# A gated-convolution kernel in a new instruction order, with the memory tokens' products contracted over 128 partitions

## The reference

```python
x = x + attention(_gn(x))     # stage 1
#   xn  = rmsnorm(x) * g1;  q, k, v = w_qkv @ xn         (4 heads of 32 rows)
#   k, v get 4 learned "memory" tokens each; q = softmax over a head's rows, k = softmax over tokens
#   context = k v^T;  out = w_out @ (context^T q) + b_out;  out = rmsnorm(out) * g2
x = x + condconv(_gn(x))      # stage 2
#   pooled = 4 x 4 means;  r = sigmoid(relu(fc(relu(rconv(pooled)))))
#   w = sum_k r[k] * expert_weight[k]      (3 experts, 3 x 3 taps, another filter for each image)
#   out = conv3x3(x, w)
```

## Time and profile before

| | us |
|---|---|
| median of 3 runs (476.15 to 477.4) | 477.28 |
| the profiled execution | 476.64 |
| its span, first to last instruction | 474.9 |
| TensorE busy | 425.4 (90%) |
| VectorE busy | 373.1 (79%) |
| ScalarE busy | 293.3 (62%) |
| GpSimd busy | 253.3 (53%) |

### The profile page before, as it was taken

The page is one execution under the profiler, slowest core; times in us unless marked ns, Lnnn a source line. Parts: engine busy times, 40 slices in busy tenths (PEclk is TensorE's granted clock), DMA queues, the critical chain, the costliest instruction groups (busy, mean ns, idle before and its releaser), DMA issues.

```text
span 474.9 us, 8615 instructions
## 1 busy us (share of the span) xinstructions
PE 425.4 (90%) x2478; PEld 357.6 (75%) x2478; DVE 373.1 (79%) x773; ACT 293.3 (62%) x903; POOL 253.3 (53%) x247
## 2 busy tenths in 40 slices
PE   2868775999999999999999999999999999999796
PEld 1757674888778787878787787878788877868575
DVE  3374969798998979797979989797979797886720
ACT  2575676566676776766666667767666667554221
POOL 4635554648283747556482837575564838242220
PEclk9969595999999999999999999999999999999899
DMA  7320224224434160626243341605252332424331
GB/s 215 129 89 2 88 90 177 91 88 149 162 129 183 58 238 16 224 88 224 88 160 152 121 188 53 239 17 221 88 221 89 124 143 89 178 77 190 134 132 44
DMA packets 18786, 61.61 MB, mean 130 GB/s; under 512 B 2992, under 2 KB 4032, under 8 KB 18752
## 3 DMA queue, kind: packets, MB, share of 16 engines
q1 hardware_dynamic: 18752, 61.21, 34.1%
HBM read 19.29 MB, written 8.39 MB: 58 GB/s over the span
## 4 chain that ended last, share of the span: by engine, by line
PE 33%; DVE 31%; issue 23%; ACT 6%; DMA 3%; SPq 1%; DVEq 1%; POOL 1%; POOLq 0%; ACTq 0%
PE ps_conv L1225 7%; PE ps_y L1189 6%; DVE w_full L1006 4%; DVE stats L907 3%; DVE q_sum L848 3%; PE ps_y L1179 3%; DVE route_terms L954 3%; ACT expert_raw L653 3%; DVE k_half L792 2%; PE ps_att L1156 2%; DMA expert_raw<-_conv_expert_weight_dram 2%; DVE y_scaled L888 2%; ACT qk L592 2%; DVE x L900 2%; PE ps_qkv L1135 2%
## 5 line engine op out<-in xcount | busy, mean ns | idle before, releaser
L592 ACT ACTIVATE qk<-ps_qkv,scale 128x256 f32<-128x256 f32 x128 | 55.0, 468 | 13.8 <-PE ps_qkv L1137 13.8
L659 ACT ACTIVATE w_hi<-w_full 128x1152 fp32r<-128x1152 f32 x16 | 18.7, 1167 | 60.6 <-DVE w_full L1012 60.6
L528 POOL TENSOR_TENSOR w_lo<-w_full,w_hi 128x1152 fp32r<-128x1152 f32 x16 | 42.6, 2662 | 23.7 <-ACT w_hi L659 13.6
L509 POOL TENSOR_TENSOR scale<-ssq,minus_half 128x8 f32<-128x8 f32 x16 | 26.2, 1637 | 44.3 <-DVE ssq L881 44.3
L1135 PE MATMUL ps_qkv<-wqk_hi,x_hi 128*128 128x256 f32 x128 | 42.4, 331 | 3.7 <-ACT qk L592 3.7
L483 POOL TENSOR_TENSOR x_lo<-x,x_hi 128x1024 fp32r<-128x1024 f32 x16 | 38.2, 2387 | 12.8 <-ACT x_hi L582 12.8
L535 POOL TENSOR_TENSOR left_hi<-zeros 128x32 fp32r<-128x32 f32 x16 | 4.0, 250 | 75.0 <-DMA right_lo<-img_lo 75.0
L633 ACT ACTIVATE y_scaled<-ps_y 128x128 f32<-128x128 f32 x128 | 33.3, 291 | 12.7 <-PE ps_y L1189 12.7
L1225 PE MATMUL ps_conv<-left_hi,w_lo 128*128 128x512 f32 (+1 forms) x96 | 39.8, 414 | 0.0
L1225 PE MATMUL ps_conv<-img_hi,w_lo 128*128 128x512 f32 x96 | 39.7, 413 | 0.0
L1225 PE MATMUL ps_conv<-img_hi,w_hi 128*128 128x512 f32 x96 | 38.5, 401 | 1.1 <-POOL w_lo L528 1.1
(11 more groups left out here) (147 smaller groups left out, 1327.7 us busy)
## 6 DMA issues: line engine op xcount, KB each, us to landing
xa<-in_x_dram SPq DMA_DIRECT2D x16, 512.0 KB, 4.0
xb<-in_x_dram SPq DMA_DIRECT2D x16, 512.0 KB, 4.8
out_dram<-expert_raw SPq DMA_DIRECT2D x16, 512.0 KB, 2.9
left_hi<-img_hi SPq DMA_DIRECT2D x16, 511.5 KB, 2.9
right_hi<-img_hi SPq DMA_DIRECT2D x16, 511.5 KB, 3.7
left_lo<-img_lo SPq DMA_DIRECT2D x16, 511.5 KB, 2.9
right_lo<-img_lo SPq DMA_DIRECT2D x16, 511.5 KB, 3.7
expert_raw<-_conv_expert_weight_dram SPq DMA_DIRECT2D x1, 1728.0 KB, 8.6
```

What stands on the lines that cost most here:

```text
L509: nc.gpsimd.tensor_tensor(scale2[:, :], ssq2[:, :], minus_half[:, :], ALU.pow).then_inc(scale2_done, 1)
L528: nc.gpsimd.tensor_tensor(w_lo[p][:, :, :].rearrange("p t o -> p (t o)"), w_full[:, :], w_hi[p][:, :, :].bitcast(F32).rearrange("p t o -> ...
L592: nc.scalar.activation(qk[:, t, :], ps_qkv[t % 2][:, 0:QK], ACT.Copy, scale=scale1[:, t:t + 1]).then_inc(qkv_done, 1)
```

## The change

Two things are changed. First, `memv_t`, `mem_ones` and `memk_exp` get 128 partitions in place of 4. GpSimd zeroes them once at the start, and only the first four partitions of `memv_t` and `memk_exp` are written later, so that the two products of the memory tokens contract over 128 partitions with zeros in 124 of them.

```diff
-        memv_t = sb("memv_t", [MEM, HID])
-        mem_ones = sb("mem_ones", [MEM, CEXT])
+        memv_t = sb("memv_t", [128, HID])
+        mem_ones = sb("mem_ones", [128, CEXT])
-        memk_exp = sb("memk_exp", [MEM, HID])
+        memk_exp = sb("memk_exp", [128, HID])
             nc.gpsimd.memset(mem_ones[:, C:CEXT], 1.0)
+            nc.gpsimd.memset(memv_t[:, :], 0.0)
+            nc.gpsimd.memset(memk_exp[:, :], 0.0)
-                nc.scalar.activation(memk_exp[:, :], memk_exp[:, :], ACT.Exp).then_inc(memk_exp_done, 1)
+                nc.scalar.activation(memk_exp[0:MEM, :], memk_exp[0:MEM, :], ACT.Exp).then_inc(memk_exp_done, 1)
-                v.tensor_tensor(memk_exp[:, :], memk_t[:, :], ps_att[0:MEM, 0:HID], ALU.subtract).then_inc(memk_sub_done, 1)
+                v.tensor_tensor(memk_exp[0:MEM, :], memk_t[:, :], ps_att[0:MEM, 0:HID], ALU.subtract).then_inc(memk_sub_done, 1)
```

Second, the `do` lines of all four `step` functions stand in another order. On GpSimd every age is one higher, which leaves the sequence of its instructions as it was. On the others the order differs within a step; two of many lines:

```diff
 # VectorE
-                do(rms1, t, p, 1)
                 do(gn2_stats, t, p, 3)
-                do(gn1_aggregate, t, p, 0)
+                do(rms1, t, p, 1)
                 do(gn2_aggregate, t, p, 3)
...
                 do(image_low, t, p, 3)
+                do(gn1_aggregate, t, p, -1)
```

More of the change, by code:

```diff
@@ L538, in step @@
             def step(t, p):
-                do(rms1, t, p, 2)
-                do(routing_products, t, p, 4)
-                do(x_scale, t, p, 2)
-                turn(inverse_deviations, t, p, 1)
-                do(gn1_shift, t, p, 1)
-                do(normalise1, t, p, 1)
-                do(rms2, t, p, 3)
-                do(image_edges, t, p, 4)
-                do(filters_low, t, p, 4)
-                do(low1, t, p, 1)
-                do(q_normalise, t, p, 2)
+                do(rms1, t, p, 3)
+                do(routing_products, t, p, 5)
+                do(x_scale, t, p, 3)
+                turn(inverse_deviations, t, p, 2)
+                do(gn1_shift, t, p, 2)
+                do(normalise1, t, p, 2)
+                do(rms2, t, p, 4)
+                do(image_edges, t, p, 5)
+                do(filters_low, t, p, 5)
+                do(low1, t, p, 2)
+                do(q_normalise, t, p, 3)
             run_steps(pool, step)
@@ L676, in step @@
             def step(t, p):
+                do(gate_exponent, t, p, 4)
+                do(qkv_evacuate, t, p, 2, 4)
+                do(qkv_evacuate, t, p, 2, 5)
                 do(filters_first, t, p, 4)
-                once(expert_evacuate, t, 2, 2)
                 do(qkv_evacuate, t, p, 2, 6)
                 do(qkv_evacuate, t, p, 2, 7)
+                do(results, t, p, 5, 0)
+                once(expert_evacuate, t, 3, 6)
                 once(expert_evacuate, t, 2, 4)
-                once(expert_evacuate, t, 2, 6)
-                once(expert_evacuate, t, 3, 8)
+                do(filters_high, t, p, 4)
+                do(q_exponent, t, p, 2)
                 do(high1, t, p, 1)
-                do(filters_high, t, p, 4)
-                do(results, t, p, 5, 0)
-                do(q_exponent, t, p, 2)
                 do(squares1, t, p, 1, 0)
@@ L699, in step @@
                 do(qkv_evacuate, t, p, 1, 0)
+                once(expert_evacuate, t, 3, 8)
                 do(qkv_evacuate, t, p, 1, 1)
@@ L1021, in step @@
             def step(t, p):
+                do(q_subtract, t, p, 2)
+                do(k_maximum, t, p, 2)
+                do(k_maximum_all, t, p, 2)
+                do(y_scale, t, p, 3)
+                do(k_subtract, t, p, 2)
                 do(q_sums, t, p, 2)
@@ L1035, in step @@
                 turn(variances, t, p, 0)
+                do(mix_evacuate, t, p, 2)
                 once(expert_evacuate, t, 1, 1)
-                do(k_sums, t, p, 2)
-                do(mix_evacuate, t, p, 2)
+                do(gn2_mean, t, p, 4)
                 once(constants, t, 0)
                 do(gn1_stats, t, p, -1)
+                once(expert_evacuate, t, 3, 7)
                 do(route_bias, t, p, 3)
+                once(expert_evacuate, t, 2, 5)
                 do(route_sums, t, p, 3)
                 do(route_relu, t, p, 3)
+                do(rms2_mean, t, p, 2)
                 do(gate_sum, t, p, 3)
-                do(rms2_mean, t, p, 2)
                 do(gate_reciprocal, t, p, 3)
                 do(gate_scale, t, p, 3)
-                do(gn2_mean, t, p, 4)
                 do(image_low, t, p, 3)
+                do(gn1_aggregate, t, p, -1)
                 do(filters_second, t, p, 3)
-                once(expert_evacuate, t, 2, 7)
+                once(expert_evacuate, t, 1, 3)
                 do(k_halves, t, p, 1)
+                do(filters_third, t, p, 3)
+                do(q_maximum, t, p, 1)
                 do(k_quarters, t, p, 1)
+                do(filters_centre, t, p, 3)
                 do(k_partial_max, t, p, 1)
-                do(filters_third, t, p, 3)
-                once(expert_evacuate, t, 1, 3)
-                do(q_maximum, t, p, 1)
-                do(filters_centre, t, p, 3)
-                do(k_maximum, t, p, 1)
-                do(q_subtract, t, p, 1)
-                do(k_maximum_all, t, p, 1)
-                once(expert_evacuate, t, 1, 5)
-                do(y_scale, t, p, 2)
-                do(k_subtract, t, p, 1)
             run_steps(dve, step)
```

73 lines of the change are left out of this document (35 added, 38 removed).

## The result

The changed kernel takes 459.14 us (median of 4 runs, 458.78 to 460.76); the kernel before took 476.71 beside it (4 runs, 474.76 to 477.4). The ratio is 0.9644, with a 95% interval of 0.9606 to 0.9683. The forecast was 456.4 and its range 449 to 468. The profiled execution of after took 460.76 with a span of 459.0, so 15.9 us of span are gone.

The account below looks back on a forecast made before the run. VectorE's loop bounds the 26.03 us step; afterwards TensorE's 24.15 does, plus 0.35 of waits: 24.5. Thirteen steps save 19.9 us, other steps 1.0: 20.9 off 476.64 gives 455.7, as median 456.4; range 449 to 468.

Parts of the forecast that it names:

- The bound changes from VectorE's loop to TensorE's own work: Steady step: VectorE's loop falls to 23.56 us, behind TensorE's own work of 24.15, which then sets the step.
- The memory tokens' products, 0.56: TensorE's two memory-token products: contracting over 128 partitions saves 0.28 us at each, 0.56 a step; bounds 0 to 0.7.
- `rms1` behind `gn2_stats`, 1.2: VectorE: statistics run while `q_normalise` holds the scaling (line 785), saving 1.2 us a step; bounds 0.4 to 1.7.
- The transposes ahead of `group_means`, 0.59, and line 1166's 0.28 in that stretch: TensorE from `group_means` to `routing`: moved transposes take 0.59 us and the memory product 0.28 off VectorE's loop.
- VectorE's rest, 0.4: VectorE between `route_bias` and the next `filters_centre` or `group_means`: reordering takes off 0.4 us a step; bounds 0 to 0.6.
- New waits, 0.35 a step: TensorE waits per step: 0.15 us for `k_exponent` at key contexts, 0.1 at `k_shift`, 0.1 for `filters_low`.
- `k_maximum_all` isn't caught: VectorE's `k_maximum_all` stays 0.2 us; the slower rival had `filters_low` hold it, 2.4 us a step, 487.6 us, chance 0.08.
- I give them 1.0 together (0 to 3): The steps before and behind the thirteen steady ones: 1.0 us gained together, range 0 to 3.
- Half is given back: Rival: close margins at `k_exponent`, `filters_low` and `q_normalise` cost 0.8 us more a step, 467 us; chance 0.15.

Follow-up runs that it names:

- the experiment: The changed kernel with the memory tokens' products over 4 partitions again: 467.99 us, ratio 0.9826, step 24.68.
- the two small edits: The kernel before, in its own order, with the 128-partition memory-token products and `rms1` behind `gn2_stats`: 456.09 us, ratio 0.9597.
- three edits off the loop's longest parts: Changed kernel, expert transposes behind first `x_transpose`, plus: xa load ahead of store, 453.19 us; `spreads` ahead of `gn2_centre`, 453.09; both with `high1` before `filters_high`, 454.15.

## Why the prediction was right

- *The bound changes from VectorE's loop to TensorE's own work*, forecast as 24.15 behind 23.56. Half of it is shown: `group_means` waited for `meanvar` in every step and doesn't any more, with experiments on both sides of the scaling's swap. That VectorE waits at `route_y` in 10 of 12 steps is no sign of it, for it did so in 11 of 12 before. TensorE's own work is at most 23.6, not 24.15. The prediction took its floor from a step by removing the two waits that the rows print; the short ones stayed in it. The step of 24.22 is set by a loop that runs through VectorE's 11.05 us from `route_bias` to `k_maximum_all` too. That edits elsewhere leave the step at 24.2 to 24.3 doesn't make 24.15 a floor. The forecast of 24.5 came so close because the work was put too high (24.15 for 23.6) and the new waits too low (0.35 for 0.6).
- *The memory tokens' products, 0.56.* 0.51 became 0.22 and 0.50 became 0.24 in the rows, 0.55 together; 0.46 in the step by the experiment. It agrees with the rule of the Trainium skill that the prediction weighed here (TensorEngine Tiling (Array Packing), "Key Properties"): the gap is gone with the contraction over 4 partitions. That a drain made it, no row shows.
- *`rms1` behind `gn2_stats`, 1.2.* 1.02 alone, 1.06 when it is taken back. The scaling stands still for 0.4 us in the step shown, as worked out. Its median of 164 ns is below what I allowed (0.8), since it now often misses `q_normalise` or its greater part (11 of the 16 take 0.2 or less).
- *The transposes ahead of `group_means`, 0.59, and line 1166's 0.28 in that stretch.* The stretch did get shorter, by 5.79 - 4.98 = 0.81 in the step shown. In time 0.59 is worth nothing, as the sum had it: it stood in VectorE's loop alone.
- *VectorE's rest, 0.4.* The rows bear it out up to `filters_centre` (0.44), and `q_subtract` ahead of `k_maximum` uses it up again (0.42). The prediction had both numbers, 1.53 before and 1.87 now from `filters_centre` to `k_maximum_all`, but not that `k_maximum_all` lies on the loop that decides.
- *New waits, 0.35 a step.* At the key contexts 0.13 in place of 0.15; taking it away gained nothing. At `k_shift` and `k_part_transpose` 0.2 in place of 0.1. For `filters_low` 0.15 in place of 0.1: in four of eleven steps the new image's first product waits for it (233.73 in the step shown, after 230.91 + 2.68 = 233.59, and 0.56 behind the product ahead of it where steps without a wait have 0.30). At `group_variances` 0.13, which the sum had not. Together 0.6. The step is 24.22 to 24.38 and not 24.5: thirteen steps gave 21.5 and not 19.9.
- *`k_maximum_all` isn't caught* (0.08 given to it). Shown with 1 column and 8. The rule of the Trainium skill (VectorE: DVE Perf Modes, "What auto-detection actually checks"), which left one column open, is decided for this operation: one column of it isn't held.
- *The step that failed: "I give them 1.0 together (0 to 3)", for all steps outside the thirteen.* They lost 5.6. The prediction had line 785's part of them in mind and passed over the experts' transposes, which the change moves ahead of image 0's `x_transpose`; the trace of before had the price in two rows of the start: `x_transpose` at 11.50, and the experts' transposes at 15.27 after a wait for their transfer, with the next work at 16.90. Image 0 behind them starts 16.90 - 11.50 = 5.4 us later, and the forecast would have been about 462. The sum came out 5.0 us too high, +1.6 in the steps and -6.6 outside them. The median missed by only 2.7, since the profiled execution of before lay 0.6 below its median and that of after 1.6 above its own.
- Within the filling steps the two small edits gain 3.9 us (60.6 to 56.7), more than the range had, and the rest of the order loses 5.0. How much of either is the clock, whose time at the lower level differs between the three, is not shown.
- *Half is given back* (467): not so in size. Two of its three margins are missed, `k_exponent`'s in seven of eleven steps by 0.2 and `filters_low`'s in four by 0.3 to 0.5. `q_normalise` ends at 237.80, and the transposes that need it begin at 237.98.

## What to carry to other kernels

When two engines are close, look for the loop that passes through both, and measure its parts from start to start: a busy share of 99% hid 0.6 us of waits in a step of 24.2. An edit is worth what it takes from that loop, so the same edit was worth 0.19 us a step ahead of the reordering and 0.46 behind it, and three edits off the loop's longest parts nothing. Price the filling steps of a new order row by row like a steady step, above all what now stands behind a transfer: a single call put too early gave back a quarter of the gain. And before a whole order is rewritten, try the two small edits that the trace names: they gave as much.

## What the runs showed of the hardware that I had not expected

VectorE's maximum of one column isn't held by a running GpSimd operation, but an equally short operation with two inputs is. In after, VectorE's second `spread` (line 772, one column, two inputs) and GpSimd around it:

```profile
93.11 2.33 DVE L772 SCALAR_TENSOR_TENSOR spread<-dev,meanvar 128x1 f32<-128x1 f32 x2 [0.25 <-issue]
```

```profile
92.94 0.62 POOL L520 TENSOR_TENSOR route_prod<-rconv_t,pooled_c 128x256 f32<-128x256 f32 x1 [1.02 <-DVE pooled_c L931]
93.53 1.89 POOL L497 TENSOR_TENSOR x_nt<-x_nt,scale 128x1024 f32<-128x1024 f32 x1
```

Two instructions that take 0.21 us each when nothing is in their way last 2.33 here. The first begins 0.17 into `route_prod` and lasts 0.47, until that is over; the second begins at 93.50, 0.03 before `x_scale` (93.53 for 1.89), and lasts 1.93, until that is over. TensorE's one long wait for `spread` (1.7 us, above) is this one, and the step lasts 25.9. In eight of the thirteen pairs from 67 to 361 us the second `spread` begins 0.04 before `route_prod` and lasts 0.68; where it begins 0.12 or more before it, it takes 0.21.

That the two-input operation is held agrees with what the Trainium skill says of the port pair (SBUF — State Buffer, "Who interferes with whom"). The opposite case doesn't: GpSimd's power of 8 columns (line 511, 1.64 us, from 246.64 in the steady step) doesn't hold VectorE's two-input `img_lo` (line 938, from 247.33 for 1.28, its usual time). It was so in 15 of 15 such pairs, and the longest of its 16 instructions takes 1285 ns. What makes that GpSimd operation different stays open.
